# A six-block transformer on one core: first rounded parts of the 16-wide attention subtracted on VectorE, filler matmuls in the low-rank blocks, and two steps moved around the 128-wide attention

## The reference, cut to what matters

```python
x = x + attn_a0(layernorm(x))    # 32 heads of 16, 8 key heads, rope, causal: program stage L0a
x = x + ffn0(layernorm(x))       # 512x512 product + one of 4 rank-8 experts: L0f
x = x + attn_b0(layernorm(x))    # one head of 128: L0b
x = x + ffn0(layernorm(x))       # L0g
x = x + attn_a1(layernorm(x))    # 32 heads of 128, 8 key heads, rope, causal: L1a
x = x + ffn1(layernorm(x))       # 16 experts, 4 per token, and a shared one: L1f
x = x + attn_b1(layernorm(x))    # as attn_a0 with other weights: L1b
x = x + ffn1(layernorm(x))       # L1g
```

## Time and profile before

| what | value |
|---|---|
| median of 3 runs | 2706.99 us (2701.44 to 2716.92) |
| the profiled execution | 2709.46 us, its span 2707.7 us |
| PE busy | 2511.6 us, 93% of the span |
| DVE, ACT, POOL busy | 1919.1, 1495.9, 876.3 us |
| mean granted PE clock | 0.967 of full speed |
| stage starts (first DVE work) | L0a 9.6, L0f 385.6, L0b 438.5, L0g 512.7, L1a 565.2, L1f 1623.9, L1b 1984.5, L1g 2358.6 |

### The profile page before, as it was taken

The page is one execution under the profiler, slowest core; times in us unless marked ns, Lnnn a source line. Parts: engine busy times, 40 slices in busy tenths (PEclk is TensorE's granted clock), DMA queues, the critical chain, the costliest instruction groups (busy, mean ns, idle before and its releaser), DMA issues. The chain is left out here.

```text
span 2707.7 us, 41931 instructions
## 1 busy us (share of the span) xinstructions
PE 2511.6 (93%) x14326; PEld 1748.2 (65%) x14326; DVE 1919.1 (71%) x3640; ACT 1495.9 (55%) x2530; POOL 876.3 (32%) x818
## 2 busy tenths in 40 slices
PE   7899989879999999999999998899968999898996
PEld 5444446758888888888888875566645444355664
DVE  6888634558776777777777778677668888376775
ACT  4778822335555555555555542566537877435663
POOL 2100214245444353434344320345411001114553
PEclk9899999989999999999999998999978999999998
DMA  4000000010000000000000004988830000149888
GB/s 179 1 1 1 1 21 1 1 51 17 24 24 17 24 25 20 24 16 24 17 24 21 17 1 145 322 213 203 180 117 1 1 1 2 48 176 315 202 199 219
DMA packets 68719, 196.23 MB, mean 72 GB/s; under 512 B 8960, under 2 KB 9728, under 8 KB 63392
## 3 DMA queue, kind: packets, MB, share of 16 engines
q1 hardware_dynamic: 47456, 144.25, 15.6%
q0 software_dynamic: 21056, 49.30, 9.6%
HBM read 153.14 MB, written 40.37 MB: 71 GB/s over the span
## 5 line engine op out<-in xcount | busy, mean ns | idle before, releaser
L1499 ACT ACTIVATE L1a_ph<-single 128x512 fp32r<-128x512 f32 (+3 forms) x384 | 174.2, 489 | 181.0 <-PE single L1584 180.3
L1490 ACT ACTIVATE L1a_probs<-pair,L1a_least 128x128 f32<-128x128 f32 (+7 forms) x256 | 189.9, 744 | 73.5 <-DVE L1a_least L1633 72.2
L1639 DVE TENSOR_TENSOR L1a_pl<-single,L1a_ph 128x512 fp32r<-128x512 f32 (+3 forms) x384 | 199.8, 550 | 42.8 <-ACT L1a_ph L1499 42.3
L1655 DVE SCALAR_TENSOR_TENSOR x<-single,L1a_rinv,x 128x512 f32<-128x512 f32 x256 | 189.7, 746 | 56.9 <-PE single L1240 56.6
L1467 POOL TENSOR_TENSOR L1a_swapped<-L1a_swapped,L1a_sin 128x512 f32<-128x512 f32 x80 | 129.3, 1617 | 301.0 <-ACT L1a_swapped L1531 301.0
L1633 DVE TENSOR_REDUCE L1a_least<-pair 128x1 f32<-128x128 f32 (+7 forms) x256 | 191.0, 752 | 42.9 <-PE pair L1573 42.3
L532 ACT ACTIVATE L0a_probsT<-pair 128x896 f32<-128x896 f32 (+2 forms) x192 | 148.9, 811 | 55.9 <-PE pair L671 44.1
L532 ACT ACTIVATE L1b_probsT<-pair 128x896 f32<-128x896 f32 (+2 forms) x192 | 148.9, 811 | 55.9 <-PE pair L671 44.1
L831 DVE CUSTOM_DVE_ANT_0 single<-single,later 128x384 f32<-128x384 f32 (+1 forms) x256 | 155.6, 646 | 21.1 <-PE single L648 20.7
L1584 PE MATMUL single<-ident,L1a_probs 128*128 128x128 f32 x1152 | 168.9, 274 | 0.4 <-ACT L1a_probs L1490 0.4
L1238 PE MATMUL single<-L1a_xh,L1a_wh 128*128 128x512 f32 x384 | 159.1, 414 | 0.0
(11 more groups left out here) (542 smaller groups left out, 7053.2 us busy)
## 6 DMA issues: line engine op xcount, KB each, us to landing
L1f_wd<-in_L1f_w SPq DMA_DIRECT2D x48, 512.0 KB
L1g_wd<-in_L1f_w SPq DMA_DIRECT2D x48, 512.0 KB
L1a_raw<-in_L1a_w SPq DMA_DIRECT2D x80, 256.0 KB, 2.6
L1f_store<-in_L1f_w SPq DMA_DIRECT2D x16, 1024.0 KB, 9.1
L1g_store<-in_L1f_w SPq DMA_DIRECT2D x16, 1024.0 KB, 9.9
sum<-L0a_pad_row SPq DMA_DIRECT2D x2, 2304.0 KB, 17.1
sum<-x SPq DMA_DIRECT2D x16, 256.0 KB
x<-sum SPq DMA_DIRECT2D x16, 256.0 KB, 6.2
```

The costliest lines, as they stand in the source:

```text
L1490: act.activation(probs[:, u % 2, 0:n], g.pair[u % 2][:, 0:n], ACT.Exp, bias=least[:, u % 4:u % 4 + 1], scale=-1.0, accum_out=rsum[:, h % 2 ...
L1499: act.activation(p_tile(ph, u, i), turned_bank(u, i), ACT.Copy).then_inc(p_high, 1)
L1639: dve.tensor_tensor(p_tile(pl, u, i), turned_bank(u, i), p_tile(ph, u, i).bitcast(F32), ALU.subtract)\
L1655: dve.scalar_tensor_tensor(out=g.x[:, t, :], in0=aux_bank(("O", h, t)), scalar=rinv[:, h % 2, t:t + 1], in1=g.x[:, t, :], op0=ALU.mult, op ...
```

## The change

`second_rest` goes from POOL's list to DVE's as a new letter `h`, with its two waits, and stands between `b` and `c` of the next tile. PE's and ACT's orders stay. In `lora_ffn` PE gets 14 + 5 + 9 matmuls of 512 bf16 columns whose result nobody reads. In `attention128` the wait for the tables with the bias scaling goes from before the loop of tiles to its round 4, and head 31's `o` steps are each followed by a wait for their own end and a `bn_stats`; L1f takes none any more.

```diff
+def keep_busy(pe, g, bank, n):
+    for _ in range(n):
+        pe.matmul(g.bank(bank), g.ident_b[:, :], g.later[:, :], start=True, stop=True)
...
     "DVE": (
-        "l l l l l l l l a b c d a b c e d g a b c e d g a b c m e d g a b c m e d g a m b c m e d g a m b m "
-        "c e d g a m b m c m d m m m m m m e m g e m g m m m m m m m m m m m m m m m m m m m m m"
+        "l l l l l l l l a b c d a b h c e d g a b h c e d g a b h c m e d g a b h c m e d g a m b h c m e d g "
+        "a m b m h c e d g a m b m h c m d m m m h m m m e m g e m g m m m m m m m m m m m m m m m m m m m m m"
     ),
     "POOL": (
-        "p p p p p p s p p"
+        "s"
     ),
...
+                def second_rest(t):
+                    dve.wait_ge(a.split1, t + 1)
+                    if t >= 2:
+                        dve.wait_ge(a.stack_ready, 2 * (t - 1))
+                    dve.tensor_tensor(a.rest1s[:, t % 2, :, :], a.rcs[:, t % 2, :, :], a.stacks[:, t % 2, :, 1, :],
+                                      ALU.subtract).then_inc(a.rest1_ready, 1)
...
@@ lora_ffn, tensor @@
+                keep_busy(pe, g, 3, 14)
                 ln_turn(pe, g, ln, 0)
                 pe.wait_ge(loaded, 48)
                 for t in range(NT + 2):
                     if t + 1 < NT:
+                        if t == 0:
+                            keep_busy(pe, g, 3, 5)
                         ln_turn(pe, g, ln, t + 1)
...
+                        if t == 0:
+                            keep_busy(pe, g, 3, 9)
                         pe.wait_ge(w_split, 1)
                         pe.wait_ge(x_split, t + 1)
...
@@ attention128, vector @@
-                dve.wait_ge(loaded, 64)
-                dve.tensor_scalar(bias[:, 2:2 + GH, :], bias[:, 2:2 + GH, :], -SCALE, None, ALU.mult).then_inc(scaled, 1)
                 for t in range(NT):
                     if t + 2 < NT:
                         ln_row(dve, g, ln, t + 2)
+                    if t == BLK:
+                        dve.wait_ge(loaded, 64)
+                        dve.tensor_scalar(bias[:, 2:2 + GH, :], bias[:, 2:2 + GH, :], -SCALE, None, ALU.mult)\
+                            .then_inc(scaled, 1)
                     turned_rows_low(dve, g, t, xh, xl, x_high, x_split)
...
+                        if h == HEADS128 - 1:
+                            dve.wait_ge(added, ADDED[s])
+                            dve.bn_stats(g.stats[:, t, :], g.x[:, t, :])
...
@@ routed_ffn, scalar and vector @@
-                ln_root(act, ln, out is not None)
+                ln_root(act, ln, True)
-                ln_stats(dve, g, ln, out is not None)
+                ln_stats(dve, g, ln, True)
```

More of the change, by code:

```diff
@@ L464, in _ @@
                 pool.memset(a.stacks[:, :, NH:NQK, 6, 0:3], 1.0).then_inc(a.slots_ready, 1)
[L465 to L471, removed]
                 def split_most(kv, c):
@@ L501, in _ @@
                 for token, n in opening16("POOL"):
-                    if token == "p":
-                        second_rest(n)
-                    elif token == "s":
+                    if token == "s":
                         split_most(0, 0)
@@ L884, in _ @@
                         rotated(n)
+                    elif token == "h":
+                        second_rest(n)
                     elif token == "e":
```

## The result

The changed kernel takes 2716.61 us (median of 20 runs, 2709.93 to 2723.14), the kernel before 2709.03 us (20 runs on the same chip, 2701.44 to 2716.98). The ratio of the runs is 1.0033, with a 95% interval from 1.0024 to 1.0042: 6.5 to 11.4 us slower, about 9. The forecast was 2712 us, 5 slower, in a range of 2700 to 2724: the time lies in it, 4.6 above the forecast, and 2.0 of these are already in the kernel before, which measures 2709.03 here and had 2706.99 there. The profiled execution has a span of 2715.9 us, 8.2 more than before. Two medians further down take in slow executions at a mean granted clock of 0.625 to 0.686 (4320.90 and 3460.02 us of the bridge, 3633.68 us of the first four moments together), which their ratios leave out.

The account below looks back on a forecast made before the run. PE was taken to bound the kernel, a DVE and ACT chain setting the time late in each opening. Terms +15.0 - 3.6 - 5.6 - 0.6 = +5.2 on the profiled 2709.46, 2712 against the median; range 2700 to 2724 us.

Parts of the forecast that it names:

- part 1: Openings in L0a and L1b: subtraction on DVE, h(6) waiting for ACT ahead of c(7); +7.5 us each, +15.0 in all.
- part 2: L0f and L0g: filler matmuls keep PE's clock up, so the first products run faster; -3.6 us, from -4.4 to 0.
- part 3: Start of L1a: DVE's wait for the tables' DMA goes, first key product comes earlier; -5.6 us, from -7.1 to -4.
- part 4: Eight moments moved from L1f to L1a's end; -0.6 us, from -4.3 to +1.3.
- The +0.7 for the clock: Each opening: PE goes to the lower clock in the longer gap; +0.7 us, between 0 and 2.
- The first rival: Openings: stalls beside POOL are what counts and h never waits long; -7.6 us in all, total 2690; chance 0.10.
- if the filler keeps the clock: L0f and L0g: condition under which the first 12 products save 1.97 and 1.61 us.
- the second rival: L0f and L0g: filler runs at the lower clock, first product +6.8 us a block; total 2726; chance 0.12.
- the third rival: L1a: ACT still waits for tables and scaling before reading the first key product; +10.8 us, total 2718; chance 0.08.
- The +1.3 ahead of p255: End of L1a: three moments before the last low part, on which PE's last weighing waits, cost +1.3 us.
- the tail, +2.4: L1a's tail: four moments, 2.8 us less the idle 0.43, cost +2.4 us.
- the -4.3 in L1f: L1f: without its eight moments the first sigmoid comes sooner after DVE's first work, as in L1g; -4.3 us.

Follow-up runs that it names:

- the bridge: Changed kernel with the opening of the kernel before, plus six more filler matmuls ending PE's list in the stages before L0f and L0g: 2701.98 us, ratio 0.9967.
- the first four moments together: Changed kernel with the opening of the kernel before, L1a's first four moments taken together after the fourth addition: 2704.78 us, ratio 0.9988.

## Why the prediction was right or wrong

| term | forecast | measured | from |
|---|---|---|---|
| part 1, two openings | +15.0 | +15.4 | stage lengths, 9 kernels against 2; whole kernel +14 |
| part 2, filler | -3.6 | -1.1 (change) | stage lengths |
| part 3, tables | -5.6 | -6.1 | distance to the first weights, 5 kernels against 9 |
| part 4, moments | -0.6 | +0.4 to +0.6 | last weights of L1a to first sigmoid of L1f |
| sum | +5.2 | +8.7 | ratio: +6.5 to +11.4 |

**Part 1, right, step by step.** h(6) was forecast at 86.0 and one later for the slip upstream, and started at 87.00; c(7), m(8), d(7) took from 87.74 to 90.9, 3.1 us as summed; h(7), forecast 91.9 and one, came at 92.98; e(6), 94.5 and one, at 95.78, 8.3 later than before. The stretched cast is gone (0.29 us instead of 1.48), and the last e is 7.6 later. The +0.7 for the clock had the right direction, as the openings have 6.8 us more at 0.50; its size was measured by nothing. That the sum came within 0.4 us of the mean is partly luck, as L0a gave 8.2 and L1b 7.2 where 7.5 was forecast for each. By the tile rows L0a and L1b do the same; that L1b shows only +5.8 between the two profiled executions is the scatter of the kernel before, whose L1b, at 374.1, was the longest of nine with that opening.

**The first rival fell for the reason given against it**: p(6) did not move. The form with every h before its e shows more: even where h never waits and nothing is stretched, nothing is gained. The rule of the Trainium skill (SBUF — State Buffer, Who interferes with whom), as the prediction quotes it, is for a DVE instruction with two SBUF inputs. It doesn't fit the cast beside which it stood, which has one; it fits the three stretched multiplications by cosine and sine, of which the first line is one in the kernel before and the second the same operation of the next tile without POOL beside it:

```profile
72.86 1.49 DVE L790 TENSOR_TENSOR L0a_rc<-L0a_qk,L0a_cos 128x128 f32<-128x128 f32 x1
...
80.43 0.28 DVE L790 TENSOR_TENSOR L0a_rc<-L0a_qk,L0a_cos 128x128 f32<-128x128 f32 x1
```

With POOL's subtraction gone none of them, nor the cast, is stretched any more. But three of the four stalls lay in time that PE's list seems to have covered, and what a stall costs can't be read from its length.

**Part 2 was mis-sized.** The step that failed is "if the filler keeps the clock". The argument, that PE was working until just before each stage, overlooked the 2.44 us between the stages, which are part of the 4.77 in the earlier trace rows. The clock fell, as the second rival said it might, but for 3.4 us and not to the end: the price was not the rival's 6.8 a block but 1 to 1.2. Against the mean of the five kernels without filler (L0f 52.7, L0g 52.4) a block gave 0.4 to 0.6 where the clock fell and 1.4 to 1.7 where it held. With the bridge the two together give 3.2 of the 3.6 forecast.

**Part 3 was right** in mechanism and size, and the third rival fell. Its sign "no wait of DVE for a DMA" held but for 0.54 us. The cost that it named at the edge of its range, POOL's weight splits beside DVE's operations, is there in four of nine kernels, 1 us each, but not in the change.

**Part 4 had the wrong sign, and was off by a microsecond.** The +1.3 ahead of p255 came as 1.2; the tail, +2.4, as 1.9 (four moments of 0.6 less the idle 0.43; the 0.1 each for the wait isn't seen); the -4.3 in L1f as -4.0. What was put at nothing is what the 1.2 do to PE: its idle pieces ahead of the last weighing grow from 0.17 and 1.62 us to 0.42, 0.44 and 1.93, the clock falls as the weighing begins, and c comes 1.5 us later still.

**L1g** is 3.9 us longer in the profiled execution, and the change has nothing there. Over the fourteen profiled kernels it is 349.1 to 357.3 us long with no order by part; the kernel before has the shortest. That 8.2 us in the spans and 8.7 in the terms agree so well is in part such chance. The forecast's sum is 3.5 us under the measured terms, 2.5 of them from part 2 and 1.0 to 1.2 from part 4.

## What to carry to other kernels

When an operation moves to another engine, its own time is often the least of it: look up when its input comes, and what stands behind it in the new list. An operation whose input is late belongs directly before its reader, behind everything that is ready; two letters in a hand-written order were worth 14 us here, eight more operations an opening on the engine nothing that could be measured. Small additions are free only where the engine is really idle: three moments ahead of the last low part delayed it by 1.2 us, and what follows by 1.5 more as the clock fell, where four of them a step later delayed neither.

## What the runs showed of the hardware

The granted clock fell in L0g in six of six kernels and in L0f in two of six, about the start of the same filler and behind the same idle time of 2.44 us of PE, and in none of six blocks where six matmuls more had cut that gap to 1.14 us. Each such fall was to 0.50 and lasted 3.4 us although PE worked throughout; without filler it lasted 10.2 us in all ten blocks. So in these kernels filler within the stage came too late for the idle time ahead of it, and the end of the stage before was the better place. That the same code gave 51.0 or 52.3 us by where the fall came also says how much of a profiled stage of 50 us is chance.

A DVE operation that starts beside one of POOL's can take almost three times as long by a difference of a tenth of a microsecond: the same normalised tile took 1.54 to 1.62 us where POOL started at most 0.07 us after it, and 0.55 where POOL started 0.18 us after it or later.
